# First pair of a graph layer: adjacency loaded once and transposed by TensorE, small vector work moved to GpSimd

## The reference

```python
h = maximum(layernorm(x), 0)
c = relu(bn1(conv1(h)))                  # 128 x 128 product
x_conv = relu(bn2(conv2(c)) + h)         # 17 taps along the nodes
s = h @ w_se.T + b_se                    # 3 columns
A = exp(-|s_n - s_m|^2) * adj
x_nmp = A @ relu(h @ w_msg.T + b_msg)
gi = concat(x_conv, x_nmp) @ w_ih.T + b_ih
gh = h @ w_hh.T + b_hh
r, z = sigmoid(gi_r + gh_r), sigmoid(gi_z + gh_z)
n = tanh(gi_n + r * gh_n)
out = x + (1 - z) * n + z * h
```

## Time and profile before

| | |
|---|---|
| median of three runs | 319.84 us |
| the profiled execution | 317.6 us |
| its span | 315.8 us |
| TensorE busy | 295.7 us, 94% |
| VectorE busy | 257.3 us, 81% |
| ScalarE busy | 180.2 us, 57% |
| GpSimd busy | 24.8 us, 8% |
| chain that ended last | PE 77%, issue 8%, DVE 6%, POOL 3%, ACT 2%, DMA 2% |
| granted TensorE clock, mean | 0.989 |

### The profile page before, as it was taken

The page is one execution under the profiler, slowest core; times in us unless marked ns, Lnnn a source line. Parts: engine busy times, 40 slices in busy tenths (PEclk is TensorE's granted clock), DMA queues, the critical chain, the costliest instruction groups (busy, mean ns, idle before and its releaser), DMA issues.

```text
span 315.8 us, 5868 instructions
## 1 busy us (share of the span) xinstructions
PE 295.7 (94%) x2042; PEld 268.6 (85%) x2042; DVE 257.3 (81%) x621; ACT 180.2 (57%) x330; POOL 24.8 (8%) x35
## 2 busy tenths in 40 slices
PE   6978679899899999999999999999999999999991
PEld 5777568699888999899988999899989998899880
DVE  6799997998999889969897889788996988664433
ACT  1766684796459651985189534965198517402320
POOL 7300300400002001100020002000110000000000
PEclk9999999999999999999999999999999999999995
DMA  7990069092085207730393009510671020002001
GB/s 198 248 196 2 1 158 224 20 207 61 2 189 131 83 2 154 152 95 3 84 200 111 6 6 220 133 45 2 142 157 36 2 60 6 3 1 69 0 25 41
DMA packets 28320, 27.45 MB, mean 87 GB/s; under 512 B 2532, under 2 KB 19956, under 8 KB 28164
## 3 DMA queue, kind: packets, MB, share of 16 engines
q1 hardware_dynamic: 27272, 26.62, 36.0%
q0 software_dynamic: 160, 0.07, 0.5%
q10 hardware_dynamic: 860, 0.40, 0.4%
HBM read 22.88 MB, written 4.19 MB: 86 GB/s over the span
## 4 chain that ended last, share of the span: by engine, by line
PE 77%; issue 8%; DVE 6%; POOL 3%; ACT 2%; DMA 2%; SPq 0%; DVEq 0%; POOLq 0%
PE bank L1127 21%; PE bank L1129 21%; PE bank L1128 21%; PE bank L1239 4%; PE bank L1208 3%; PE bank L1304 2%; PE bank L1182 2%; DMA place<-in_x 2%; POOL rstd L350 1%; PE bank L1229 1%; ACT x_norm L409 1%; PE bank L1220 1%; POOL bn_rstd L367 1%; DVE stats L664 1%; DVE h_lo L695 0%
## 5 line engine op out<-in xcount | busy, mean ns | idle before, releaser
L1127 PE MATMUL bank<-a_hi,w_hi 128*128 128x248 f32 (+2 forms) x328 | 93.7, 286 | 6.2 <-DVE w_lo L866 3.6
L1129 PE MATMUL bank<-a_hi,w_lo 128*128 128x248 f32 (+2 forms) x328 | 91.0, 278 | 0.0
L1128 PE MATMUL bank<-a_lo,w_hi 128*128 128x248 f32 (+2 forms) x328 | 91.0, 278 | 0.0
L1127 PEld LDWEIGHTS bank<-a_hi,w_hi 128*128 128x128 f32 x328 | 61.9, 189 | 8.0 <-issue 5.2
L1128 PEld LDWEIGHTS bank<-a_lo,w_hi 128*128 128x128 f32 x328 | 62.0, 189 | 0.6
L1129 PEld LDWEIGHTS bank<-a_hi,w_lo 128*128 128x128 f32 x328 | 61.8, 188 | 0.0
L350 POOL TENSOR_TENSOR rstd<-var_eps,halves 128x8 f32<-128x8 f32 (+1 forms) x9 | 14.1, 1571 | 199.6 <-DVE var_eps L681 199.6
L1127 PE MATMUL bank<-h_hi,w_hi 128*128 128x512 f32 (+1 forms) x66 | 28.0, 424 | 1.0 <-ACT h_hi L436 0.6
L1129 PE MATMUL bank<-h_hi,w_lo 128*128 128x512 f32 (+1 forms) x66 | 26.2, 397 | 0.0
L1128 PE MATMUL bank<-h_lo,w_hi 128*128 128x512 f32 (+1 forms) x66 | 26.2, 397 | 0.0
L484 ACT ACTIVATE nmp_hi<-bank 128x512 fp32r<-128x512 f32 x16 | 9.5, 592 | 28.7 <-PE bank L1239 28.7
(11 more groups left out here) (151 smaller groups left out, 656.2 us busy)
## 6 DMA issues: line engine op xcount, KB each, us to landing
adj_in<-in_adj SPq DMA_DIRECT2D x64, 256.0 KB, 6.2
place<-in_x SPq DMA_DIRECT2D x32, 64.0 KB, 2.3
out<-x_slot SPq DMA_DIRECT2D x32, 64.0 KB
out<-place SPq DMA_DIRECT2D x30, 64.0 KB
x_slot<-in_x SPq DMA_DIRECT2D x28, 64.0 KB, 2.4
place<-in_L_gnn_conv_w SPq DMA_DIRECT2D x1, 1088.0 KB, 7.2
place<-in_L_gnn_w_ih SPq DMA_DIRECT2D x1, 384.0 KB, 6.5
x_slot<-in_x ACTq DMA_DIRECT2D x4, 64.0 KB, 2.3
```

What stands on the lines that cost most here:

```text
L1127: pe.matmul(out, w_hi[:, mat, :], hi, start=start, stop=False)
L1128: pe.matmul(out, w_hi[:, mat, :], lo, start=False, stop=False)
L1129: final = pe.matmul(out, w_lo[:, mat, :], hi, start=False, stop=stop)
```

## The change

The first step's adjacency is loaded once per group, its rows permuted by the DMA to (r, v) on the partitions (`load_first_adj`, four DMAs of 64 KB). ScalarE copies it with its columns permuted into the free second quarter of the buffer (`first_adj_columns`), TensorE transposes the copy four times 128 x 128 into banks B_HN and B_N (`first_adj_transposes`), and ScalarE copies the bank to `adj_T` (`first_adj_out`). VectorE's two `adj_transposed(0, k)` go. `gru_transposes(0)` and `(1)` use the same banks and go behind `a1` on TensorE, with a wait for both `adj_T`. VectorE's `norm_columns(1)` and the four recurrent-bias instructions go to GpSimd, in its order between the second norm's pow and the next layer norm. On VectorE `h_low(0, 1)` and `norm_columns(0)` change places. Later steps are as before. New semaphores `adjc_ready`, `adjtr_done` and `bn2_chain` are declared in the part left out.

```diff
@@ -286,6 +286,12 @@
+    def load_first_adj(k):
+        src = adj[k * GB:(k + 1) * GB].rearrange("b (v r) m -> r v b m", r=4)
+        for r in range(4):
+            sp.dma_start(adj_in[k][r * VN:(r + 1) * VN, :, 0:N], src[r]).then_inc(adj_in_sem[k], 16)
     def store_y(s, b):
@@ -299,8 +305,8 @@
     sp.dma_start(ih_nat, w_ih.rearrange("(a o) i -> o a i", a=3)).then_inc(gruw_in, 16)
-    load_adj(0, 0)
-    load_adj(0, 1)
+    load_first_adj(0)
+    load_first_adj(1)
     for k in range(2):
@@ -365,6 +371,18 @@
         pool.tensor_tensor(bn_rstd[:, col], bn_rstd[:, col], halves[:, col], ALU.pow).then_inc(bn_rstd_ready, 1)
+    col = slice(1, 2)
+    pool.wait_ge(bn_rstd_ready, 4)
+    pool.tensor_tensor(bn_scale[:, col], vcol[:, 4:5], bn_rstd[:, col], ALU.mult).then_inc(bn2_chain, 1)
+    pool.wait_ge(bn2_chain, 1)
+    pool.tensor_tensor(bn_ms[:, col], vcol[:, 6:7], bn_scale[:, col], ALU.mult).then_inc(bn2_chain, 1)
+    pool.wait_ge(bn2_chain, 2)
+    pool.tensor_tensor(bn_shift[:, col], vcol[:, 5:6], bn_ms[:, col], ALU.subtract).then_inc(bn2_chain, 1)
+    pool.tensor_tensor(gru_s[:, :], vcol[:, 8:10], vcol[:, 11:13], ALU.add).then_inc(gru_chain, 1)
+    pool.tensor_scalar(gru_b[:, 2:3], vcol[:, 13:14], 0.5, None, ALU.mult).then_inc(gru_chain, 1)
+    pool.tensor_copy(gru_b[:, 3:4], vcol[:, 10:11]).then_inc(gru_chain, 1)
+    pool.wait_ge(gru_chain, 3)
+    pool.tensor_scalar(gru_b[:, 0:2], gru_s[:, :], 0.5, None, ALU.mult).then_inc(gru_chain, 1)
     for t in range(1, NP):
@@ -459,6 +477,17 @@
+    def first_adj_columns(k):
+        act.wait_ge(adj_in_sem[k], 16 * 4)
+        act.activation(adj_in[k][:, :, N:2 * N].rearrange("n b (r v) -> n b r v", r=4),
+                       adj_in[k][:, :, 0:N].rearrange("n b (v r) -> n b r v", r=4), ACT.Copy
+                       ).then_inc(adjc_ready, 1)
+    def first_adj_out(k):
+        act.wait_ge(adjtr_done, k + 1)
+        act.activation(adj_T[k][:, :], bank[(B_HN, B_N)[k]][:, :], ACT.Copy).then_inc(adjT_ready, 1)
     def message_relu(t):
@@ -487,7 +516,7 @@
         if s == 0:
-            act.wait_ge(bn_chain, 6)
+            act.wait_ge(bn2_chain, 3)
             act.wait_ge(w_lo_ready, splits_until("g1"))
@@ -539,6 +568,8 @@
         a1_high_phases(0)
+        first_adj_columns(0)
+        first_adj_columns(1)
         last_tap_copy()
@@ -546,6 +577,8 @@
         weights_high("a1")
+        first_adj_out(0)
+        first_adj_out(1)
         weights_high("b")
@@ -907,21 +940,16 @@
         dve.tensor_copy(w_ms[:, D:D + NSE], vcol[:, 14:NVEC]).then_inc(w_ms_ready, 1)
-        dve.tensor_tensor(gru_s[:, :], vcol[:, 8:10], vcol[:, 11:13], ALU.add).then_inc(gru_chain, 1)
-        dve.tensor_scalar(gru_b[:, 2:3], vcol[:, 13:14], 0.5, None, ALU.mult).then_inc(gru_chain, 1)
-        dve.tensor_copy(gru_b[:, 3:4], vcol[:, 10:11]).then_inc(gru_chain, 1)
-        dve.wait_ge(gru_chain, 3)
-        dve.tensor_scalar(gru_b[:, 0:2], gru_s[:, :], 0.5, None, ALU.mult).then_inc(gru_chain, 1)
-    def norm_columns(i):
-        col = slice(i, i + 1)
-        dve.wait_ge(vcol_ready, i + 1)
-        dve.wait_ge(bn_rstd_ready, 2 * i + 2)
-        dve.tensor_tensor(bn_scale[:, col], vcol[:, 4 * i:4 * i + 1], bn_rstd[:, col], ALU.mult).then_inc(bn_chain, 1)
-        dve.wait_ge(bn_chain, 3 * i + 1)
-        dve.tensor_tensor(bn_ms[:, col], vcol[:, 4 * i + 2:4 * i + 3], bn_scale[:, col], ALU.mult).then_inc(bn_chain, 1)
-        dve.wait_ge(bn_chain, 3 * i + 2)
-        dve.tensor_tensor(bn_shift[:, col], vcol[:, 4 * i + 1:4 * i + 2], bn_ms[:, col], ALU.subtract).then_inc(bn_chain, 1)
+    def norm_columns():
+        col = slice(0, 1)
+        dve.wait_ge(vcol_ready, 1)
+        dve.wait_ge(bn_rstd_ready, 2)
+        dve.tensor_tensor(bn_scale[:, col], vcol[:, 0:1], bn_rstd[:, col], ALU.mult).then_inc(bn_chain, 1)
+        dve.wait_ge(bn_chain, 1)
+        dve.tensor_tensor(bn_ms[:, col], vcol[:, 2:3], bn_scale[:, col], ALU.mult).then_inc(bn_chain, 1)
+        dve.wait_ge(bn_chain, 2)
+        dve.tensor_tensor(bn_shift[:, col], vcol[:, 1:2], bn_ms[:, col], ALU.subtract).then_inc(bn_chain, 1)
@@ -933,8 +961,8 @@
         h_low(0, 0)
-        norm_columns(0)
         h_low(0, 1)
+        norm_columns()
         dve.wait_ge(msgT_done, 1)
@@ -947,7 +975,6 @@
         messages(0)
-        norm_columns(1)
         weights_low("g0")
@@ -970,12 +997,10 @@
         weights_low("b0")
-        adj_transposed(0, 0)
         weights_low("b1")
...
         parity_part(0, 1)
-        adj_transposed(0, 1)
         masked_edges(0, 1)
@@ -1321,13 +1346,23 @@
+    def first_adj_transposes(k):
+        pe.wait_ge(adjc_ready, k + 1)
+        if k == 0:
+            pe.wait_ge(taps_ready, 3)
+            pe.wait_ge(taps_ready_dve, 2)
+        for b in range(GB):
+            tr = pe.transpose(bank[(B_HN, B_N)[k]][:, b * N:(b + 1) * N],
+                              adj_in[k][:, b, N:2 * N], ident[:, :])
+        tr.then_inc(adjtr_done, 1)
     def gru_transposes(i):
...
         pe.wait_ge(gruw_in, 32)
-        pe.wait_ge(taps_ready, 3)
-        pe.wait_ge(taps_ready_dve, 2)
         if i == 2:
             pe.wait_ge(edge_ready, 2)
+        else:
+            pe.wait_ge(adjT_ready, 2)
         natural = [hh_nat[:, gate, :] for gate in range(3)]
@@ -1377,10 +1412,12 @@
         distances(0, 1)
+        first_adj_transposes(0)
+        first_adj_transposes(1)
+        conv2_product(0, "a0")
+        conv2_product(0, "a1")
         gru_transposes(0)
         gru_transposes(1)
-        conv2_product(0, "a0")
-        conv2_product(0, "a1")
         conv2_product(0, "b")
```

More of the change, by code:

```diff
@@ L156, in gnn_block @@
             "vecs_in", "msgw_in", "c1_in", "c2_in", "gruw_in", "bias_in"))
-        bn1_in, vecs_in_pool = sem("bn1_in"), sem("vecs_in_pool")
+        adjc_ready, adjtr_done, bn1_in, vecs_in_pool = sem("adjc_ready"), sem("adjtr_done"), sem("bn1_in"), sem("vecs_in_pool")
         x_in = [[sem(f"x_in{i}_{k}") for k in range(2)] for i in range(4)]
@@ L161, in gnn_block @@
         const_set, dve_const = sem("const_set"), sem("dve_const")
-        vecT_done, vcol_ready, bn_rstd_ready, bn_chain, gru_chain = (sem(n) for n in (
-            "vecT_done", "vcol_ready", "bn_rstd_ready", "bn_chain", "gru_chain"))
+        vecT_done, vcol_ready, bn_rstd_ready, bn_chain, bn2_chain, gru_chain = (sem(n) for n in (
+            "vecT_done", "vcol_ready", "bn_rstd_ready", "bn_chain", "bn2_chain", "gru_chain"))
         tapT_done, taps_ready_dve, taps_ready = (sem(n) for n in ("tapT_done", "taps_ready_dve", "taps_ready"))
```

## The result

The changed kernel takes 316.25 us (median of 7 runs, 314.86 to 317.11), the kernel before 319.66 us (317.31 to 320.52, 7 runs). The ratio is 0.990, 95% interval 0.9861 to 0.9938, which is 2 to 4.4 us less. Forecast were 317.4 us and 2.5 us less. By the time alone, 316.25 us lies nearer to the rival "all arrives" (315.8 us) than to the forecast; what tells them apart is in the traces.

The account below looks back on a forecast made before the run. TensorE bounds the steady part, so only its earlier leaving of the first pair counts, with VectorE the releaser there. 0.86 + 0.77 = 1.63 us at the aggregation, plus 0.85, gives 2.5 us: 317.4 us, range 315.2 to 319.6.

Parts of the forecast that it names:

- all arrives: Rival: all that VectorE sheds arrives at TensorE, 4.0 us gained, 315.8 us; chance 0.20.
- Step 2: Second norm's columns leave VectorE at 20.86 to 21.32 us, directly ahead of w_lo for g0 and g1: 0.46 us.
- Step 1: Four recurrent-bias instructions leave VectorE near 14 us, h_low(0, 1) goes ahead of norm_columns(0): 0.4 us, between 0.28 and 0.69.
- Step 3: GpSimd does the seven moved instructions behind the second norm's pow: hidden, VectorE not held up, 0 us.
- The rival in which VectorE waits: VectorE waits for GpSimd, 1.4 us lost up to 20.5 us; gain 1.1 us, 318.7 us; chance 0.16.
- Step 4: ScalarE's two column copies before L425, about 0.612 us each (bounds 0.5 to 1.1), fit its idle time, 0.4 us spare.
- the sign named for it: In the new trace the copies take 0.6 to 0.7 us and ScalarE's L425 still waits for VectorE.
- Step 5: TensorE's eight transposes, 1.1 us, before a0 and six between a1 and b go into existing waits: cost nothing.
- the 0.6 at most that was named as a sign: In the new trace TensorE shows no wait before b above 0.6 us.
- Step 6: VectorE's two removed transposes: first, before w_lo of b1, gives nothing; second removes TensorE's 0.77 us wait before the first aggregation.
- Step 7: Second pair's adjacency loads earlier, x lands sooner, TensorE's wait for dist_r before dist_transposes(1) goes: 0.85 us.

Follow-up runs that it names:

- vec_part: Kernel before with only norm_columns(1) and the recurrent biases moved to GpSimd and h_low(0, 1) put ahead of norm_columns(0): 318.31 us, ratio 0.9983.
- after: First profile of the changed kernel, nothing altered: span 314.1 us; the changed kernel's median is 316.25 us.
- adj_part: Changed kernel with norm_columns(1), the recurrent biases and the order of h_low and norm_columns(0) put back, adjacency change kept: 316.64 us, ratio 0.9918.
- the two first profiles: First profile of the kernel before and first profile of the changed kernel, nothing altered: spans 315.8 and 314.1 us.
- taps_alone: Kernel before and changed kernel, each with SyncE waiting for conv_w to land before its further loads: 318.2 and 315.09 us, ratios 0.9974 and 0.9891.
- before_taps_alone: Kernel before with SyncE waiting for conv_w to land before asking for the second pair's x and all that follows: 318.2 us, ratio 0.9974.
- before_2: Kernel before, unaltered, profiled once more: one execution, 318.95 us.
- before_3: Kernel before, unaltered, profiled yet again: one execution, 318.31 us.
- no_copies: Changed kernel without ScalarE's two column copies, so the first pair's mask is permuted: 316.25 us, ratio 0.9903.
- t_first: Changed kernel with a spare VectorE transpose where adj_transposed(0, 0) stood, before w_lo of b1: 316.63 us, ratio 0.9911.
- late_second_adj: Changed kernel with the second pair's adjacency loads held back until w_lo of b0 and of gru0: 317.17 us, ratio 0.994.

## Why the prediction was right, step by step

- **Steps 1 and 2.** Step 2, forecast 0.46 us, is 0.45 to 0.49 (`vec_part`, and `after` beside `adj_part`). Step 1, forecast 0.4, is 0.37 between the two first profiles and 0.44 between the two of `taps_alone`, but 0 or less where the old kernel's pow takes 0.58 us (3.53 and 3.57 us in the old kernel, 3.64 in the new). In these two the four recurrent-bias instructions still stand on VectorE, and the stretch is none the longer: they cost nothing there. What the step gives comes with the long pow, for which the old order makes `h_low(0, 1)` and with it TensorE wait (0.28 us in the earlier trace rows, 0.27 in `before_taps_alone`, none at that place in `before_2` and `before_3`). The prediction names no pow here; that its size came out is in part luck of the profile that it was read from.
- **Step 3.** Right: VectorE's sums stay at 0.70 us, GpSimd's three were done at 16.4, its seven at 18.6 us, well inside the bounds. The rival in which VectorE waits is refuted by the stretch of `vec_part`, 0.45 us shorter and not longer. The port rule of the Trainium skill (SBUF — State Buffer, "Who interferes with whom"), by which the one that starts first makes the other wait in full, agrees with the traces where VectorE starts first: `gru_s` beside the sum 0.66 us against 0.20, the pow 1.12 against 0.58. Where the pow starts first it does not: `h_lo` begins 0.03 to 0.41 us behind it in four profiles, while the pow still runs, and is not held up. Here the measurement decides: this is the direction of which the prediction had no row. It says nothing of longer GpSimd instructions.
- **Step 4.** The size was wrong, 1.09 us each for 0.612, at the upper bound that I took from VectorE's transpose, and so was the sign named for it: `last_tap_copy` does not wait for VectorE but starts 0.4 us later behind the first tap transposes (12.01 us, for 11.59 in `no_copies`), and `g_scaled` makes `a` wait. The nearest row by shape read PSUM, the copies read SBUF. That it costs nothing all the same was right (`no_copies`), and VectorE's `w_lo` of `a` was not held up, as foreseen. That `a` itself starts some 0.4 us late was not foreseen; it goes into the wait that TensorE has before `a0` in `no_copies`, 0.48 us, and no longer here.
- **Step 5.** Right: eight transposes end before `a0`, which starts at 30.48 behind VectorE's `w_lo`; the six use 0.82 us of the wait for `b`. What is left of it is 0.75 us, not the 0.6 at most that was named as a sign.
- **Step 6.** Right in both: the first transpose nothing (`t_first`; 1.10 us idle in its place), the second 0.90 us for the forecast 0.77. The rival "all arrives", 4.0 us, falls with it. 0.77 was the modelled idle time before the aggregation; without a wait the aggregation starts 0.17 us before the modelled end of the product ahead of it (46.08 us, against 45.97 + 0.28), so the idle time undercounts by that much.
- **Step 7.** The mechanism was right (`late_second_adj`), the term was mis-sized: 0.85 us, where the stretch shortens by 1.08 us between the first profiles and by 1.81 to 2.12 against `before_2`, `before_3` and `before_taps_alone`. It was read from one execution, the one with the shortest of these waits.
- **Not foreseen.** With the new loads the tap weights land later. Where TensorE waits for them, the taps start at 12.2 to 12.9 us in place of 11.4, up to 1.5 us of the gain, and 1.2 us between the two first profiles. So the sum of 2.5 us is in part luck: step 7 was put 0.2 to 1.3 us too low and this term at nothing, and the two errors have opposite signs. By the table 0.46 + 0.9 + (1.1 to 2.1) - (0 to 1.5) + (0 to 0.4) spans 1.0 to 3.9 us; the forecast 2.5 lies in it, and so does most of the measured 2.0 to 4.4 us.

Open is how the adjacency loads, later and smaller, slow a transfer that was asked for at 3.5 us. SyncE's eight x loads, next in its queue, took 4.04 to 4.71 us to issue in the four profiles with the old loads and 4.83 to 5.69 in the eight with the new, and all of these come before any changed instruction of that queue. Neither the layout in memory nor the code that is fetched was varied.

## What to carry to other kernels

Where an engine has no idle time over 20 us, what is taken from it is worth something only up to the next engine's work that is due at the same moment: the value of each removed instruction is to be looked for at the very instruction behind it, and its own time is no measure of it (here 1.10 us were worth nothing and 1.11 us were worth 0.9). A wait on a transfer should be read in several executions before it goes into a sum, while a stretch in which only engines wait for engines can be taken from one, unless two engines start almost together in it: a start 0.03 us earlier or later decided here between 0.58 and 1.12 us. A buffer freed early can be worth more through the later loads that it moves out of the way (1.1 to 2.1 us here) than through the instruction that was removed (0.9 us).

## What the runs showed of the hardware

- A ScalarE copy of 128x512 from SBUF to SBUF takes 1.09 us when it reads with a step of 4 elements and 1.08 us when it writes with one of 32, and 0.63 us in a row (`weights_high`, L395); a read from PSUM with a step of 4 took 0.612.
- VectorE's transpose of 128x512 took 0.70 us with a step of two elements from x, and 1.10 us with a step of four from the adjacency.
- GpSimd's pow on 128x1 for the first norm takes 1.12 or 1.13 us when VectorE's `h_lo` (128x512, two inputs in SBUF) starts with it or 0.01 us ahead (nine profiles), and 0.58 us when the pow starts 0.03 us or more ahead or after `h_lo` (five). `h_lo` takes 0.69 or 0.70 us in all fourteen.
- A load of 1088 KB landed 7.2 to 8.1 us after its issue in the four profiles with the old adjacency loads behind it, 8.6 to 9.3 us in the eight with the new, and 6.6 and 6.8 us in the two in which nothing was issued on its queue until it had landed.
